# Another order for the same operations on four engines of a two-layer attention and FFN kernel

## The reference

```python
x = x + _L0_xattn_ref(_layernorm(x), ctx_768, ...)   # 16 heads of 16, q, k, v, softmax over 77 keys, w_o
x = x + _L0_ffn_ref(_layernorm(x), ...)              # only expert 0 counts: relu(x@w1)@w2, 256-1024-256, then a layernorm
x = x + _L1_xattn_ref(_layernorm(x), ctx_768, ...)   # one head, width 256, own layernorms on x and context
x = x + _L1_ffn_ref(_layernorm(x), ...)              # each position's token goes through one of 8 matrices, chosen by position
```

## Time and profile before

| | |
|---|---|
| median of 3 runs | 313.17 us (312.77 to 313.40) |
| span of the profiled execution | 314.0 us |
| mean granted TensorE clock | 0.932 of full |
| busy: PE, DVE, ACT, POOL | 267.9, 254.8, 181.7, 157.3 us |
| instructions: PE, DVE, ACT, POOL | 2080, 664, 606, 157 |

### The profile page before, as it was taken

One profiled execution on the slowest core, in us unless ns is written; L12 is line 12 of the kernel. 1 busy time (PEld: TensorE's weight loads), 2 busy tenths in 40 slices (PEclk: granted clock), 3 DMA queues, 4 the chain that ended last, 5 costly groups with the idle time before them and its releaser, 6 DMA issues.

```text
span 314.0 us, 6283 instructions
## 1 busy us (share of the span) xinstructions
PE 267.9 (85%) x2080; PEld 232.0 (74%) x2080; DVE 254.8 (81%) x664; ACT 181.7 (58%) x606; POOL 157.3 (50%) x157
## 2 busy tenths in 40 slices
PE   2954958977999998999999989999989999878960
PEld 2743937763999698689789959988878988666850
DVE  2998998972889999998997789899899986875640
ACT  2468628526368857478695857775754471454510
POOL 2253640275225878821652263268766653164854
PEclk9995596995999999999999999999999999997995
DMA  6922010240000372100001000011110000000222
GB/s 177 336 72 77 8 42 25 67 142 27 3 0 3 115 222 51 29 24 2 2 0 35 2 0 2 33 52 51 37 36 0 2 0 1 3 0 34 87 78 73
DMA packets 8797, 15.32 MB, mean 49 GB/s; under 512 B 1270, under 2 KB 6813, under 8 KB 8509
## 3 DMA queue, kind: packets, MB, share of 16 engines
q1 hardware_dynamic: 6845, 9.68, 9.2%
q0 software_dynamic: 1920, 5.25, 5.9%
HBM read 11.77 MB, written 3.15 MB: 48 GB/s over the span
## 4 chain that ended last, share of the span: by engine, by line
PE 37%; DVE 29%; issue 15%; POOL 12%; ACT 3%; DVEq 1%; DMA 1%; POOLq 0%; SPq 0%; ACTq 0%
PE PB L256 16%; PE PB L249 7%; PE PB L460 5%; DVE SM L598 3%; POOL SM L1220 3%; DVE SX L649 3%; DVE SM L609 3%; PE S L365 3%; PE S L377 2%; POOL out_x L1282 2%; DVE WD L837 2%; PE PB L327 2%; POOL RAW L1275 2%; DVE XN L701 2%; POOL HL L1254 2%
## 5 line engine op out<-in xcount | busy, mean ns | idle before, releaser
L1220 POOL TENSOR_TENSOR SM<-SM,nhalf 128x2 f32<-128x2 f32 x40 | 29.4, 737 | 98.4 <-DVE SM L604 97.9
L1060 ACT ACTIVATE E<-S,SX 128x77 f32<-128x77 f32 x128 | 39.5, 340 | 16.8 <-DVE SX L652 16.6
L256 PE MATMUL PB<-XTH,W1H 128*128 128x256 f32 x128 | 38.3, 299 | 3.9 <-issue 2.2
L1254 POOL TENSOR_TENSOR HL<-HF,HH 128x512 fp32r<-128x512 f32 x26 | 34.5, 1335 | 13.6 <-DVE HH L682 12.0
L1094 ACT ACTIVATE HF<-PB,cols 128x256 f32<-128x256 f32 x64 | 26.8, 473 | 20.9 <-PE PB L256 20.6
L256 PE MATMUL PB<-W2H,HH 128*128 128x256 f32 x128 | 37.9, 296 | 1.1 <-DVE HL L688 1.1
L256 PE MATMUL PB<-XTH,W1L 128*128 128x256 f32 x128 | 36.4, 284 | 0.0
L256 PE MATMUL PB<-XTL,W1H 128*128 128x256 f32 x128 | 36.4, 284 | 0.0
L256 PE MATMUL PB<-W2H,HL 128*128 128x256 f32 x128 | 35.8, 280 | 0.0
L256 PE MATMUL PB<-W2L,HH 128*128 128x256 f32 x128 | 35.8, 279 | 0.0
L460 PE MATMUL PB<-WD,XP 128*128 x120 | 29.9, 402 | 0.8 <-issue 0.8
(11 more groups left out here) (188 smaller groups left out, 778.3 us busy)
## 6 DMA issues: line engine op xcount, KB each, us to landing
RAW<-in_w SPq DMA_DIRECT2D x4, 512.0 KB, 5.0
WD<-in_WD SPq DMA_DIRECT2D x2, 1024.0 KB
X<-in_x SPq DMA_DIRECT2D x4, 256.0 KB, 7.1
x<-X SPq DMA_DIRECT2D x4, 256.0 KB, 2.2
bc<-in_rows SPq DMA_DIRECT2D x1, 768.0 KB, 7.3
RAW<-in_w_q SPq DMA_DIRECT2D x1, 256.0 KB, 4.2
Wo<-in_w_o SPq DMA_DIRECT2D x1, 256.0 KB, 7.8
RAW<-in_WqT SPq DMA_DIRECT2D x1, 256.0 KB
```

Source lines behind the costliest of these rows:

```text
L256: t = e.matmul(dst, a, b, start=first and j == 0, stop=last and j == n - 1)
L1060: t = e.activation(Ei[:, h * NK:(h + 1) * NK], P[:, at:at + NK], ACT.Exp, bias=SX[:, i, 2, k:k + 1], accum_out=SX[:, i, 1, k:k + 1])
L1220: e.tensor_tensor(sm(K, g, 9), sm(K, g, 8), nhalf[:, :], ALU.pow).then_inc(s["rs" + K], 1)
L1254: e.tensor_tensor(HL[:, hs, :], HF[:, (4 * g + j) % 3, :, :], f(HH[:, hs, :]), ALU.subtract).then_inc(s["hlP"], 1)
```

## The change

All four lists (PE, DVE, ACT, POOL) have the same pieces in another order: 246, 275, 249 and 130 calls. The PSUM places of the PE pieces are chosen anew. `pv(g, 1)` and the later quarters of `w2` no longer repeat their bank, but look it up where their first piece was put; this changes no instruction. SP's list and all pieces' bodies stay. What the argument speaks of stands here; the orders' middle parts are cut.

```diff
                 t.then_inc(s["tE"], 1)
 
-            def pv(g, a, p):
+            def pv(g, a, p=None):
                 w.wait_ge(s["vb"], g // 4 + 1)
                 w.wait_ge(s["et"], 4 * g + 2 + a + 1)
-                P = hold(("pv", g), ("B", p), ("o", g + 1)) if a == 0 else PB[p]
+                P = hold(("pv", g), ("B", p), ("o", g + 1)) if a == 0 else PB[place["pv", g][1]]
 
                 for c in range(2):
                     for n in range(4):
@@ -409,12 +409,12 @@
                               [((W1H[:, c, fs], W1L[:, c, fs]), (XTH[:, 3, c, :], XTL[:, 3, c, :])) for c in range(2)])
                 t.then_inc(s["w1"], 1)
 
-            def w2(g, i, h, p):
+            def w2(g, i, h, p=None):
                 w.wait_ge(s["wlo"], 5)
                 for j in range(4):
                     hh_here(w, g, j)
                     hl_here(w, g, j)
-                P = hold(("w2", g), ("B", p), ("y", g + 1)) if i + h == 0 else PB[p]
+                P = hold(("w2", g), ("B", p), ("y", g + 1)) if i + h == 0 else PB[place["w2", g][1]]
                 ts = slice(i * 128, (i + 1) * 128)
                 t = three(P[:, i * 256:(i + 1) * 256],
                           [((HH[:, j, ts], HL[:, j, ts]), (W2H[:, j, :], W2L[:, j, :])) for j in range(4 * h, 4 * h + 4)],
...
-            keys(0); tA(0, 1); vmat(2); q(0, 3); vrep(0, 0); vrep(1, 1); sc(0, 0, 0, 0); sc(0, 0, 1, 1); r_scores(2)
-            tA(1, 3); sc(0, 1, 0, 1); sc(0, 1, 1, 0); q(1, 0); r_rank(1); tE(0, 0, 0, 0); tA(2, 2); tE(0, 0, 1, 1)
-            tE(0, 1, 0, 0); tE(0, 1, 1, 1); sc(1, 0, 0, 0); sc(1, 0, 1, 1); pv(0, 0, 3); pv(0, 1, 3); sc(1, 1, 0, 1)
-            q(2, 0); wo(0, 1); sc(1, 1, 1, 0); tE(1, 0, 0, 1); f_turn(3); tE(1, 0, 1, 1); f_kv(0, 2); r_perm(1)
-            f_kv(1, 3); tB(0, 0); sc(2, 0, 0, 0); tE(1, 1, 0, 1); f_m(1); tE(1, 1, 1, 1); w1(0, 0, 2); w1(0, 1, 0)
-            w1(0, 2, 2); pv(1, 0, 0); pv(1, 1, 0); sc(2, 0, 1, 1); w1(0, 3, 2); wo(1, 0); sc(2, 1, 0, 0); f_q(3)
-            w2(0, 0, 0, 2); tA(3, 0); w2(0, 0, 1, 2); w2(0, 1, 0, 2); w2(0, 1, 1, 2); sc(2, 1, 1, 1); tB(1, 1)
...
-            w1(4, 1, 2); w1(4, 2, 3); pv(5, 0, 0); cp(2, 1); w1(4, 3, 2); tE(6, 0, 0, 0); sc(6, 1, 0, 1)
-            pv(5, 1, 0); tC(3, 3); co(2); sc(6, 1, 1, 0); wo(5, 2); cs(3, 0); w2(4, 0, 0, 3); w2(4, 0, 1, 3)
-            w2(4, 1, 0, 3); sc(7, 0, 0, 0); cp(3, 2); tE(6, 0, 1, 1); tB(5, 0); w2(4, 1, 1, 3); tE(6, 1, 0, 1)
...
-            tB(7, 1); w2(6, 1, 1, 0); tD(2, 2); cs(5, 3); w1(7, 0, 1); w1(7, 1, 0); w1(7, 2, 3); cp(5, 1)
-            w1(7, 3, 2); tD(3, 0); pr(0, 0, 3); co(5); pr(0, 1, 0); w2(7, 0, 0, 2); w2(7, 0, 1, 2); w2(7, 1, 0, 2)
-            w2(7, 1, 1, 2); tC(6, 1); tD(4, 3); cs(6, 0); pr(0, 2, 2); cp(6, 1); pr(0, 3, 0); co(6); pr(0, 4, 2)
-            tD(5, 1); tC(7, 3); cs(7, 1); pr(0, 5, 3); tD(6, 0); cp(7, 1); co(7); pr(0, 6, 0); pr(0, 7, 2)
-            pr(1, 0, 3); pr(1, 1, 1); tD(7, 0); pr(1, 2, 2); pr(1, 3, 3); pr(1, 4, 0); pr(1, 5, 1); pr(1, 6, 2)
-            pr(1, 7, 3)
+            keys(0); vmat(1); tA(0, 0); q(0, 2); vrep(0, 0); vrep(1, 1); r_scores(3); sc(0, 0, 0, 0); sc(0, 0, 1, 1)
+            tA(1, 2); sc(0, 1, 0, 1); q(1, 0); sc(0, 1, 1, 0); sc(1, 0, 0, 0); tE(0, 0, 0, 1); r_rank(0)
+            tE(0, 0, 1, 1); tA(2, 3); r_perm(2); tE(0, 1, 0, 0); tE(0, 1, 1, 1); pv(0, 0, 0); pv(0, 1); sc(1, 0, 1, 1)
+            sc(1, 1, 0, 0); q(2, 2); wo(0, 0); sc(1, 1, 1, 1); tA(3, 3); tE(1, 0, 0, 1); sc(2, 0, 0, 0)
+            sc(2, 0, 1, 1); q(3, 0); tB(0, 3); tE(1, 0, 1, 0); tE(1, 1, 0, 0); w1(0, 0, 3); w1(0, 1, 0); pv(1, 0, 3)
+            tE(1, 1, 1, 1); sc(2, 1, 0, 0); w1(0, 2, 0); pv(1, 1); sc(2, 1, 1, 1); tA(4, 0); w1(0, 3, 2); wo(1, 3)
+            tE(2, 0, 0, 1); tE(2, 0, 1, 0); f_turn(1); sc(3, 0, 0, 1); sc(3, 0, 1, 0); w2(0, 0, 0, 1); w2(0, 0, 1)
+            tB(1, 3); tE(2, 1, 0, 0); w2(0, 1, 0); w1(1, 0, 3); w2(0, 1, 1); tE(2, 1, 1, 1); w1(1, 1, 0); pv(2, 0, 2)
...
+            w2(4, 1, 1); pv(6, 0, 2); tE(6, 1, 1, 1); tC(2, 0); w1(5, 0, 3); w1(5, 1, 1); sc(7, 0, 1, 0); cs(2, 0)
+            w1(5, 2, 3); cp(1, 1); sc(7, 1, 0, 0); sc(7, 1, 1, 1); co(1); pv(6, 1); w1(5, 3, 3); cp(2, 0); tC(3, 1)
+            wo(6, 2); cs(3, 1); co(2); tE(7, 0, 0, 1); w2(5, 0, 0, 1); w2(5, 0, 1); cp(3, 2); w2(5, 1, 0); w2(5, 1, 1)
+            tE(7, 0, 1, 1); co(3); tE(7, 1, 0, 0); tE(7, 1, 1, 1); tC(4, 1); tB(6, 0); pv(7, 0, 2); pv(7, 1); cs(4, 1)
+            w1(6, 0, 0); wo(7, 2); w1(6, 1, 0); w1(6, 2, 2); w1(6, 3, 0); cp(4, 2); tC(5, 1); tB(7, 3); co(4)
+            cs(5, 1); w1(7, 0, 3); w2(6, 0, 0, 0); w2(6, 0, 1); w2(6, 1, 0); tD(0, 1); w1(7, 1, 3); w2(6, 1, 1)
+            w1(7, 2, 1); pr(0, 0, 2); tD(1, 1); cp(5, 3); w1(7, 3, 0); co(5); pr(0, 1, 1); tD(2, 0); w2(7, 0, 0, 2)
+            w2(7, 0, 1); pr(0, 2, 1); tD(3, 3); w2(7, 1, 0); w2(7, 1, 1); tC(6, 1); pr(0, 3, 3); cs(6, 1); pr(0, 4, 2)
+            pr(0, 5, 3); pr(0, 6, 2); tC(7, 1); cp(6, 3); tD(4, 0); cs(7, 1); co(6); pr(0, 7, 2); pr(1, 0, 1)
+            cp(7, 3); tD(5, 0); co(7); tD(6, 0); pr(1, 1, 1); pr(1, 2, 0); tD(7, 1); pr(1, 3, 3); pr(1, 4, 1)
+            pr(1, 5, 3); pr(1, 6, 1); pr(1, 7, 3)
...
-            setup(); mask(); stats("A", 0); apply("A", 0); kf(); lo("A", 0); kbl(0); r_sign(); kbl(1); vs()
-            stats("A", 1); ql(0); vb(0); vb(1); apply("A", 1); smax(0, 0, 0); smax(0, 0, 1); stats("A", 2)
-            r_expert(); smax(0, 1, 0); smax(0, 1, 1); ssum(0, 0, 0); lo("A", 1); apply("A", 2); stats("A", 3)
-            ssum(0, 0, 1); f_stats(); ssum(0, 1, 0); ssum(0, 1, 1); ql(1); r_position(); apply("A", 3)
-            smax(1, 0, 0); smax(1, 0, 1); o(0); lo("A", 2); ssum(1, 0, 0); smax(1, 1, 0); f_norm(); ssum(1, 0, 1)
-            ssum(1, 1, 0); x1(0); smax(1, 1, 1); stats("B", 0); ssum(1, 1, 1); apply("B", 0); ql(2); r_index()
-            f_kv(0); smax(2, 0, 0); lo("B", 0); r_pairs(); hh(0, 0); hh(0, 2); o(1); f_kv(1); hlD(0, 1); hh(0, 3)
...
+            setup(); mask(); stats("A", 0); apply("A", 0); kf(); kbl(0); lo("A", 0); stats("A", 1); vs(); r_sign()
+            apply("A", 1); ql(0); vb(0); smax(0, 0, 0); smax(0, 0, 1); lo("A", 1); stats("A", 2); smax(0, 1, 0)
+            ssum(0, 0, 0); ssum(0, 0, 1); ql(1); smax(0, 1, 1); apply("A", 2); r_expert(); ssum(0, 1, 0)
+            ssum(0, 1, 1); smax(1, 0, 0); r_position(); stats("A", 3); lo("A", 2); r_index(); apply("A", 3)
+            ssum(1, 0, 0); kbl(1); o(0); smax(1, 1, 0); smax(1, 0, 1); ql(2); x1(0); smax(1, 1, 1); stats("B", 0)
+            ssum(1, 0, 1); ssum(1, 1, 0); smax(2, 0, 0); ssum(1, 1, 1); apply("B", 0); stats("A", 4); lo("A", 3)
+            f_stats(); ssum(2, 0, 0); apply("A", 4); stats("A", 5); lo("B", 0); ql(3); smax(2, 0, 1); f_norm()
+            hh(0, 0); ssum(2, 0, 1); smax(2, 1, 0); stats("A", 6); o(1); smax(2, 1, 1); hh(0, 2); hlD(0, 1); vb(1)
+            x1(1); hh(0, 3); stats("B", 1); hlD(0, 3); ssum(2, 1, 0); ssum(2, 1, 1); apply("B", 1); smax(3, 0, 1)
+            smax(3, 0, 0); lo("A", 4); lo("B", 1); apply("A", 5); r_pairs(); y(0); ssum(3, 0, 0); ssum(3, 0, 1)
+            hh(1, 0); o(2); smax(3, 1, 0); stats("Y", 0); hh(1, 2); x1(2); x2(0); stats("B", 2); ssum(3, 1, 0)
...
-            apply("A", 0); rep(); w_hi(0); hi("A", 0); qh(0); kba(0); w_hi(1); kba(1); ex(0, 0, 0); apply("A", 1)
-            ex(0, 0, 1); w_hi(2); w_hi(3); hi("A", 1); ex(0, 1, 0); ex(0, 1, 1); apply("A", 2); rr(0, 0, 0); qh(1)
-            rr(0, 0, 1); w_hi(4); et(0, 0, 0); rr(0, 1, 0); hi("A", 2); et(0, 0, 1); rr(0, 1, 1); et(0, 1, 0)
-            et(0, 1, 1); ex(1, 0, 0); rr(1, 0, 0); ex(1, 0, 1); ex(1, 1, 0); qh(2); rr(1, 0, 1); et(1, 0, 0); f_ct()
-            ex(1, 1, 1); et(1, 0, 1); apply("B", 0); rr(1, 1, 0); hi("B", 0); rr(1, 1, 1); et(1, 1, 0); et(1, 1, 1)
...
+            rep(); apply("A", 0); w_hi(0); kba(0); hi("A", 0); kba(1); qh(0); w_hi(1); apply("A", 1); w_hi(2)
+            hi("A", 1); ex(0, 0, 0); ex(0, 0, 1); qh(1); rr(0, 0, 0); ex(0, 1, 0); rr(0, 0, 1); ex(0, 1, 1)
+            apply("A", 2); et(0, 0, 0); rr(0, 1, 0); w_hi(3); ex(1, 0, 0); rr(0, 1, 1); et(0, 0, 1); hi("A", 2)
+            et(0, 1, 0); et(0, 1, 1); w_hi(4); apply("A", 3); rr(1, 0, 0); qh(2); ex(1, 0, 1); ex(1, 1, 0); hi("A", 3)
+            ex(1, 1, 1); rr(1, 0, 1); et(1, 0, 0); ex(2, 0, 0); apply("B", 0); rr(1, 1, 0); qh(3); hi("B", 0)
+            et(1, 0, 1); rr(1, 1, 1); apply("A", 4); rr(2, 0, 0); et(1, 1, 0); hf(0, 0); ex(2, 0, 1); hf(0, 1)
+            hhA(0, 1); et(1, 1, 1); rr(2, 0, 1); hf(0, 2); ex(2, 1, 0); hf(0, 3); hi("A", 4); ex(2, 1, 1); et(2, 0, 0)
+            et(2, 0, 1); f_ct(); rr(2, 1, 0); rr(2, 1, 1); apply("B", 1); hi("B", 1); ex(3, 0, 0); ex(3, 0, 1)
...
-            setup(); rs("A", 0); w_lo(0); r_iota(); rs("A", 1); bo(0); w_lo(1); rs("A", 2); w_lo(2); f_rs()
-            rs("A", 3); bo(1); w_lo(3); bo(2); w_lo(4); rs("B", 0); gx(4); gx(5); gx(6); gx(7); hlP(0, 0); hlP(0, 2)
```

(27 more changed lines are left out.)

116 lines of the change are left out of this document (45 added, 71 removed).

## The result

The changed kernel takes 316.24 us (median of 5 runs, 315.98 to 316.80); in the same call the kernel before took 313.40 (312.77 to 314.56). The ratio is 1.0082, 95% interval 1.0057 to 1.0106: slower, where 310.4 and a gain were forecast. Run again on two chips, the changed kernel gave 1.0027 (0.9976 to 1.0078) and 1.0110 (1.0058 to 1.0162). So its time is some 0.3 to 1.1% above that of before; in the second of the three calls the difference is not clear of the noise, and no call shows a gain.

What follows compares the result with a forecast made beforehand. TensorE was taken to bound the middle, with gains possible at the two ends. Terms -1.5 (front), +0.6, -1.3 (middle) and -0.6 (tail) summed to -2.8 us, from 313.17 to a median of 310.4, range 305.5 to 316.5.

Steps and rivals of the forecast that it cites:

- Front: Up to the first w2 of group 0: w2 starts at 80.7 to 83.6 us instead of 82.62, counted as -1.5 us.
- both pauses: Two late starts of ScalarE's hf in the old front, 6.4 us together, which the prediction could not explain from the trace.
- lag: Time of a piece less the work queued before it; forecast for TensorE 33.3 at first w2, 43.8 at its end.
- My rival: ScalarE's unexplained hf pauses come again in the new front, holding hh, hlD and w2: 315.6 us, chance of slower 0.30.
- Middle: After the first w2: +0.6 us where VectorE leads, then -1.3 us from smaller leads and waits that go.
- No wait at tC(3): Sign of being right: its 1.50 us wait for apply C3 goes, with 8 us more of TensorE's work ahead of it.
- The leads of 16 to 17.5: How far VectorE's queue to needed pieces exceeds TensorE's, w1(1,0) to tB(2); 11 to 12 before; counted in the +0.6 us.
- The moved bs gathers: Eight on POOL between rs B4 and rs Y3, 8 x 1.3 us; x2(3) may stand 6 us; costed at nothing.
- From group 6 to w2(7): Stretch ending at the first w2 of group 7, where TensorE's lag was forecast at 39.0, against 41.2 before.
- Tail: From the first w2 of group 7 to TensorE's end: lag grows 4.8 instead of 5.4 us, counted as -0.6 us.
- the waits for cs, cp and co: Late TensorE waits, 4.0 us together before, claimed to mostly go because pr pieces now stand between them.
- slower: Outcome given chance 0.30: ScalarE's pauses come again, or L837 is held 6 us; 315.6 us.

Runs made afterwards that it cites:

- before_pa01: Kernel before with pa(0,0) and pa(0,1) ahead of hh(7,3), hlD(7,1), hlD(7,3) on VectorE; ratio to the kernel before 1.0133.
- hl7_first: Changed kernel with hh(7,3), hlD(7,1), hlD(7,3) directly behind hh(7,2) on VectorE; ratio to the kernel before 1.0159.
- hl7_mid: Changed kernel with hh(7,3), hlD(7,1), hlD(7,3) behind apply D2, y(7) and its statistics ahead of pa(0,2), pr(0,2) in bank 0; ratio to the kernel before 1.0275.
- chain_first: Changed kernel with all four lists and the banks rewritten from w2(7) on, the late chain's pieces ahead of pa and pr pieces; ratio to the kernel before 1.0362.
- old_front_96: Order of before for what before had begun by 96 us, then the changed order; ratio to the kernel before 1.0500.
- tc7_between: Changed kernel with tC(7) in bank 0 and between pr(0,5) and pr(0,6); no usable ratio: one time of 314.5, five from 319.3 to 320.2.

## Why the prediction was wrong

The miss is 316.24 less 310.4, 5.8 us. On the scale of the table 1.9 of it lies between the profiled execution and the median, 3.0 in the front, -2.4 between the front and w2(7), and 3.2 in the tail.

*From the profiled execution to the median* (1.9). I took the span of 314.0 as 0.8 above the median. As a time it was 2.3 above it. The changed kernel's profiled execution is 0.56 above its own median. 1.7+0.8-0.56 = 1.94.

*Front* (forecast -1.5: wrong). I forecast w2(0,0,0) at 80.7 to 83.6. It came at 85.25, 85.5 and 83.3. Step by step: tA(1) 22.55 (forecast 20.5) and q(1) 26.59 (24.0), since the first w_lo, the smax of the scores and half clock from 20 us on made the start slower; r_position was held by one w_lo as worked out (L839 2.10 us; it ended at 42.2, 5.6 long, against 6.05); wo(0) at 50.51 as forecast (50.6); and then a second instruction, L650, was held 2.41 beside the last w_lo, which I had not counted, and gave tE(1,0,0) at 56.92 (54.8), q(3) at 63.41 (61). The Trainium skill ("SBUF — State Buffer", Who interferes with whom) counts a tensor_scalar among the instructions that can take both ports, and the 2.41 us agree.

And what it was measured against comes and goes. Of five traces with the old front two have both pauses (82.6 and 83.2 for the first w2), two have one of 4.9 (81.0 and 81.4), one has none (76.1). With none, and the late order of before, TensorE would end at 303.4-6.5 = 296.9, the span be 307.5 and the time 309.2; the quickest executions of before in the last call, at 309.03 to 309.33 and a clock of 0.946 to 0.957, fit that, but none of them was profiled. So at the first w2 the old front is 6 to 8 us better than the new one when the signals come in time (lag 28.3 against 34.4 to 36.5), and about level when they don't. By the first w1 of group 6 most of that is gone without any pause: before_pa01 stands at a lag of 32.7 there, the changed kernel at 32.2 to 36.7. The 5.6 us that the changed kernel is ahead there in the table are less than what the pauses cost before (39.7 against 32.7) and no gain of the new order. Against an execution without pauses the whole loss lies behind that w1. My rival had it the wrong way round: I feared the pauses for the new order, and none of the 15 traces with the new front has them at the hf of group 0. The step that failed is the base of the sum: I had seen 6.4 us that no row explained, and took them as part of the old order.

*Middle* (forecast +0.6, then -1.3: right in sign, too small). The lag did not grow; it fell from 36.3 to 34.1 up to group 6. No wait at tC(3), none at w1(6,0). The leads of 16 to 17.5 that I feared held. The moved bs gathers cost nothing in ten of the sixteen traces that have them in the new place. In six, all of two chips, a transpose's signal reached ScalarE late while they ran, and 2.1 us were lost; the trace of hl7_first:

```profile
160.97 0.31 ACT L1069 ACTIVATE RR<-SX 128x128 f32<-128x128 f32 x1
163.19 0.28 ACT L1080 ACTIVATE RT<-S 128x128 f32<-128x128 f32 x1 [1.91 <-remote]
```

*From group 6 to w2(7)* (in the forecast 39.0, measured 39.6). The sum is nearly right by two errors that cancel: 3 us better up to group 6, and then 5.5 of growth where I had counted no wait. VectorE is busy 30.8 us of the 38 from 224 to 262, before 34.6: its list there has pieces whose input isn't ready, and hh(7,3) behind x2(6) and a pa.

*Tail* (forecast -0.6, 4.8 in place of 5.4: measured 8.0, 9.1 and 7.9). This is the largest failed step of the sum, 3.2 us in the first trace. I had said that the waits for cs, cp and co go because pr pieces stand between them. They do go. In their place the pr pieces wait: 2.40 at pr(0,5), 0.7 at pr(0,7), 1.44 at pr(1,3) (forecast 1.5), and after the stand of 3.13 and that of 2.40 the clock was at half, 0.87 on average from 260 to 280 where before had 1.00. Behind TensorE's end all is as forecast (10.7); the first and the last of POOL's eight output issues in its timeline, to set against the earlier trace rows:

```profile
301.59 1.04 POOL L1279 DMA_INDIRECT out_x<-X,SI  x1 [6.03 <-DVE X L750]
...
310.52 0.96 POOL L1279 DMA_INDIRECT out_x<-X,SI  x1 [0.30 <-issue]
```

That the late order loses is shown, by traces with either front. Which of its places is to blame is not settled: eight kernels that each took away one or several of its waits show no gain (one of them without a usable ratio), and where one wait went others of up to 3.5 us came. The profile puts these down to VectorE and to ScalarE by turns; that VectorE's list reaches the next piece too late behind all of them is my reading and not shown. Every pa of the first half has 0.75 us of standing (0.74 to 0.77) between its two instructions, but in both orders alike, so it doesn't tell them apart. Whether the pa pieces begun early are the cause was tried only in part (hl7_mid, chain_first), without a gain.

Of the chances, 0.30 stood on slower, and the time lies within the range of 305.5 to 316.5 by 0.3 us, but by other mechanisms than the one I named.

## What to carry to other kernels

Put a profiled execution among the timed ones before a sum is made from it: add what lies around the span, compare, and ask which waits in it have no cause in the order; profile the kernel before a second and third time, on another chip, to see whether they stay. What is won against a wait that comes and goes is not won. Where two engines are both nearly full, one list cannot be judged by the waits of the other: a piece moved on TensorE must be moved with its partner on VectorE and its PSUM bank, and a wait that is taken away is worth something only if nothing behind it is later still. A lead won in the middle has to be followed to the last output.

## What the runs showed of the hardware

- In nine of twenty traces a matmul's semaphore was counted up 1.2 to 5.6 us after the matmul's modelled end, and ScalarE, which waited for it, stood 1.7 to 4.9 us; in the eleven others, among them one with the same lists up to there, it did not. It happened while POOL issued eight gathers (61 to 72 us in the old front, 157 to 175 us in the changed order; 172 to 186 in old_front_96). The same nine traces miss 23 to 54 of 1346 semaphore events, the others none to two. No run tells cause from company.
- Seven VectorE instructions of 2 to 64 elements a partition lasted 2.0 to 6.2 us beside POOL tensor operations in the first traces of the two kernels, each ending within 0.1 us of one, where the same kind takes 0.15 to 0.22 alone. The one of 6.24 stood through four POOL operations that followed one another without a gap (the earlier trace rows shows two of them). Counted against the median of their operation and shape, 23 instructions in the changed kernel lost over half a microsecond, 23 us together, all of them beside a POOL operation; before 26 with 33.
- In the traces of the two kernels VectorE stands 0.74 to 0.77 us between the two instructions of a pa in the first half and 0.14 to 0.15 in the second. The code differs there only in a `value_load` of the offset, which the second half doesn't repeat, so that load costs about 0.6 us (an estimate from these two).
- The front starts in one of two ways in the changed order: the first scores stand at 18.7 to 19.6 us where the granted clock fell to half at 20.4 us or later, and at 20.1 to 21.0 where it had fallen earlier (first at 13.3 to 19.6); in one trace, tc7_between, at 24.5 with the clock at full. Between the first and the third trace of the changed kernel the difference of 1.5 us is 2.0 at the first w2 and 1.9 at TensorE's end.
